# Feed-forward result read by VectorE straight from PSUM in the last residual sum of a decoder layer

## What is computed

```python
x = _layernorm(x + _L0_attn_ref(x, ...))
x = _layernorm(x + _L0_xattn_ref(x, ctx, ctx, decay))
x = _layernorm(x + _L0_ffn_ref(x, W_fc, W_proj))

def _L0_ffn_ref(x, W_fc, W_proj):
    h = jnp.einsum('bsd,hd->bsh', x, ternary(W_fc))      # 512 -> 2048
    h = jnp.square(jax.nn.relu(h))
    hn = h * rsqrt(mean(h * h) + eps)                    # over the 2048
    return jnp.einsum('bsh,dh->bsd', hn, ternary(W_proj))  # 2048 -> 512
```

## Time and profile before

| | |
|---|---|
| median of 3 runs | 1288.41 us (1281.94 to 1293.75) |
| the profiled execution | 1287.73 us |
| its span, first to last instruction | 1285.7 us |
| TensorE (PE) busy | 1116.7 us, 87% of the span |
| VectorE (DVE) busy | 941.3 us, 73% |
| ScalarE (ACT) busy | 587.3 us, 46% |
| GpSimd (POOL) busy | 202.5 us, 16% |
| mean granted TensorE clock | 0.941 of 2.4 GHz |

### The profile page before, as it was taken

One profiled execution on the slowest core, in us unless ns is written; L12 is line 12 of the kernel. 1 busy time (PEld: TensorE's weight loads), 2 busy tenths in 40 slices (PEclk: granted clock), 3 DMA queues, 4 the chain that ended last, 5 costly groups with the idle time before them and its releaser, 6 DMA issues.

```text
span 1285.7 us, 21818 instructions
## 1 busy us (share of the span) xinstructions
PE 1116.7 (87%) x7424; PEld 879.2 (68%) x7424; DVE 941.3 (73%) x1932; ACT 587.3 (46%) x906; POOL 202.5 (16%) x202
## 2 busy tenths in 40 slices
PE   5988989898989897724589997998989989999995
PEld 4766767676767674413368786787877878778784
DVE  4238788888888896788458678586795867958746
ACT  4323243434343434011166554565565665655673
POOL 3111003030303132300430201003020030110000
PEclk8989999999999998856699998999999999999998
DMA  7466666777767577633561021101210112100001
GB/s 277 126 180 148 170 145 203 148 196 155 192 151 198 120 196 218 163 86 62 184 222 41 1 66 66 51 14 65 65 65 31 34 65 65 65 1 1 33 1 66
DMA packets 184339, 139.40 MB, mean 108 GB/s; under 512 B 140128, under 2 KB 152416, under 8 KB 180192
## 3 DMA queue, kind: packets, MB, share of 16 engines
q1 hardware_dynamic: 113120, 113.57, 32.8%
q10 hardware_dynamic: 71168, 25.17, 7.9%
HBM read 82.09 MB, written 52.43 MB: 105 GB/s over the span
## 4 chain that ended last, share of the span: by engine, by line
PE 50%; DVE 26%; ACT 9%; issue 6%; DMA 5%; SPq 3%; POOL 1%; ACTq 0%; DVEq 0%; POOLq 0%
PE ps_s L779 13%; PE ps_f L765 12%; PE ps_f L569 9%; PE ps_o L716 5%; PE ps_s L591 5%; DVE w_pos L1204 3%; SPq L386 2%; DVE row_sum L1130 2%; ACT h_sb L1000 2%; DMA w_in<-in_L_ffn_W_fc 2%; DVE h_acc L1330 2%; DVE sc L1113 2%; DVE sc L1120 2%; DVE row_max L1116 2%; DVE st L1107 1%
## 5 line engine op out<-in xcount | busy, mean ns | idle before, releaser
L765 PE MATMUL ps_f<-x2h,w 128*128 128x512 f32 x512 | 203.9, 398 | 0.2 <-issue 0.2
L779 PE MATMUL ps_s<-w,hh 128*128 128x512 f32 x500 | 201.5, 403 | 0.0
L765 PE MATMUL ps_f<-x2l,w 128*128 128x512 f32 x512 | 199.9, 390 | 0.0
L779 PE MATMUL ps_s<-w,hl 128*128 128x512 f32 x500 | 199.6, 399 | 0.0
L1319 DVE TENSOR_TENSOR hl<-h_sb,hh 128x512 fp32r<-128x512 f32 x128 | 92.1, 720 | 116.0 <-ACT hh L1004 114.3
L569 PE MATMUL ps_f<-xth,wh 128*128 128x512 f32 x384 | 156.9, 409 | 1.6 <-DVE xtl L1099 1.6
L569 PE MATMUL ps_f<-xth,wl 128*128 128x512 f32 x384 | 151.8, 395 | 0.0
L569 PE MATMUL ps_f<-xtl,wh 128*128 128x512 f32 x384 | 151.7, 395 | 0.0
L591 PE MATMUL ps_s<-qbd,k 128*32 128x128 f32 x2048 | 128.1, 412 | 19.8 <-DVE o_sb L1163 14.1
L994 ACT ACTIVATE r_sb<-ps_f 128x512 f32<-128x512 f32 x128 | 76.2, 595 | 124.8 <-PE ps_f L765 124.7
L1514 POOL TENSOR_TENSOR xb<-xb,bob 128x512 f32<-128x512 f32 x32 | 66.3, 2101 | 411.4 <-DMA xb<-in_x 411.4
(11 more groups left out here) (145 smaller groups left out, 1941.8 us busy)
## 6 DMA issues: line engine op xcount, KB each, us to landing
xa<-in_x SPq DMA_DIRECT2D x8, 1024.0 KB, 5.6
q_scr<-f_sb ACTq DMA_DIRECT2D x32, 256.0 KB, 2.4
k_scr<-f_sb ACTq DMA_DIRECT2D x32, 256.0 KB, 3.9
v_scr<-f_sb ACTq DMA_DIRECT2D x32, 256.0 KB, 3.0
w_scr<-w_st SPq DMA_DIRECT2D x32, 256.0 KB, 4.9
k<-k_scr SPq DMA_DIRECT2D x8, 1024.0 KB, 5.5
qbd<-q_scr SPq DMA_DIRECT2D x128, 64.0 KB, 3.5
v<-v_scr SPq DMA_DIRECT2D x64, 128.0 KB, 6.0
```

Source lines behind the costliest of these rows:

```text
L765: last = nc.tensor.matmul(ps_f[:, j % 2, :], w1[:, k, j * P:(j + 1) * P], xx[:, k, :], start=(k == 0 and xx is x2h), stop=(k == KC - 1 and ...
L779: last = nc.tensor.matmul(ps_s[:, t, :], a[:, j % 4, t * P:(t + 1) * P], w2[:, j, :], start=(j == 0 and a is hh), stop=(j == HC - 1 and a ...
```

## The change

ScalarE's four copies of `ps_s` to `res` at the end of each pass are dropped, and with them the semaphore `f2_ev`. VectorE's `add_hidden` reads `ps_s` itself. For this it waits for the last down group of the pass before (`f2_ps`, in the last pass `f2_tile` of the tile) and, at tile 0, for the write of the output before that one (`out_wr`). TensorE's first down group of a pass waits for the four sums (`o1_done`) in place of the four copies. The four sums of a pass stand in steps 0 (tiles 0 and 1) and 1 (tiles 2 and 3) in place of steps 1 and 3. Pass 1 is written out on all engines, and the loop runs over passes 2 to 5.

```diff
@@ phase_b, and the same on SyncE's queue
             body(0, True, False, True)
-            with eng.Fori(1, NSB - 2) as i:
+            body(1, True, True, True)
+            with eng.Fori(2, NSB - 2) as i:
                 body(i, True, True, True)
@@ TensorE, down
                 if j == 0 and later(i):
-                    pe.wait_ge(f2_ev, at(i, TT, 0))
+                    pe.wait_ge(o1_done, at(i, TT, 0))
@@ ScalarE, end of body_b
-                if prep:
-                    act.wait_ge(f2_ps, at(i, HC, HC))
-                if fin:
-                    act.wait_ge(out_wr, 16 * i)
-                for t in range(TT):
-                    if not prep:
-                        act.wait_ge(f2_tile, t + 1)
-                    nc.scalar.activation(res[:, t, :], ps_s[:, t, :], ACT.Copy).then_inc(f2_ev, 1)
@@ VectorE, add_hidden
-                v.wait_ge(f2_ev, at(i, TT, t + 1))
-                nc.vector.scalar_tensor_tensor(out=res[:, t, :], in0=res[:, t, :], scalar=h_rs[:, t:t + 1],
+                if isinstance(i, int) and i == NSB - 1:
+                    v.wait_ge(f2_tile, t + 1)
+                elif t == 0:
+                    v.wait_ge(f2_ps, at(i, HC, HC))
+                if t == 0 and not (isinstance(i, int) and i == 0):
+                    v.wait_ge(out_wr, 16 * i)
+                nc.vector.scalar_tensor_tensor(out=res[:, t, :], in0=ps_s[:, t, :], scalar=h_rs[:, t:t + 1],
                                                in1=x2c[:, t, :], op0=ALU.mult, op1=ALU.add).then_inc(o1_done, 1)
@@ VectorE, body_b
-                        if j in (1, 3):
-                            add_hidden(i - 1, j - 1)
-                            add_hidden(i - 1, j)
+                        if j in (0, 1):
+                            add_hidden(i - 1, 2 * j)
+                            add_hidden(i - 1, 2 * j + 1)
```

More of the change, by code:

```diff
@@ L263, in program @@
         f2_ps = sem("f2_ps")
-        f2_ev = sem("f2_ev")
         f2_tile = sem("f2_tile")
@@ L515, in _ @@
             body_b(0, True, False)
-            with sp.Fori(1, NSB - 2) as i:
+            body_b(1, True, True)
+            with sp.Fori(2, NSB - 2) as i:
                 body_b(i, True, True)
```

## The result

| | before | changed |
|---|---|---|
| median of the compared runs | 1285.31 us | 1304.59 us |
| lowest to highest | 1281.94 to 1293.75, 4 runs | 1301.74 to 1307.99, 4 runs |
| profiled execution | 1287.73 us | 1303.08 us |
| its span | 1285.7 us | 1301.2 us |
| mean granted TensorE clock | 0.941 | 0.938 |

The ratio is 1.0135, 95% interval 1.0099 to 1.017: the change makes the kernel 1.35% slower (the two medians stand 19.3 us, 1.5%, apart). The forecast was 1300.0 us, 1293 to 1306.

A forecast was written before the change was run, and what follows sets the result against it. A feed-forward pass was taken to last TensorE's work plus its waits, the one long wait being 3.2 us at step 15. 1287.7 + 6.2 (`kv` at six borders) + 6.0 (last pass) = 1299.9, so 1300 us, range 1293 to 1306.

The forecast's parts named there:

- The two waits of the sum: TensorE's waits on `kv` at six borders, 6.2 us, and on the sums in the last pass, 6.0 us with clock loss.
- What it removes: 32 ScalarE copies of 0.6 us: worth 0.1 us per border, nothing at the very end.
- The read from PSUM at 0.74 us: VectorE's sums reading PSUM: 0.74 us each, as from SBUF, bounds 0.68 and 0.80; 1.7 us over seven borders either way.
- The down group of a loop pass: Step 3: sums done at 900.71, TensorE comes at 900.89, so the new wait is hidden by 0.2 us.
- `kv` 1.1 and 0.9 us late at six borders: Step 3's context transposes wait for `kv`: 1.1 us at four loop borders, 0.9 at two straight ones, 6.2 us.
- The wait at step 15 unchanged: TensorE's 3.2 us wait for `x2l` stays, as VectorE's chain is started by TensorE's step 11 and shifts along.
- The last pass: TensorE's first down group waits 4.1 us for the sums, then loses 1.9 us to a lower clock: 6.0 us.
- gone 0.20: Rival: pass 1 loses its collision of VectorE with GpSimd's bias additions, total 1295.3 us; chance 0.20.
- one more 0.12: Rival: one more collision of VectorE and GpSimd, in another pass, total 1304.5 us; chance 0.12.
- Absorbed: Rival: step 15's wait ends by something not tied to TensorE, six borders cost nothing, 1293.7 us; chance 0.07.
- faster: Rival: fewer sums in step 3 bring `x2l` forward, 2.8 us in five passes, 1.2 in the sixth, 1278.5 us; chance 0.04.
- clock at each border: Rival: 1.1 us more waiting lowers the clock at six borders, 1.8 us each, 1311 us; chance 0.05.

The follow-up runs named there:

- The kernels with the copies dropped and the costs taken away: Changed kernel, `kv` ahead of `h_sq`, GpSimd's bias additions held: ratio 0.9954; with output norm at step 4 and copies kept for pass 6 too: 0.9757.
- changed with the additions held: Changed kernel with GpSimd's four bias additions held until VectorE's last `x2l`: 1295.92 us, ratio 1.0062 to the kernel before.
- the kernels with `kv` in time: Among them the changed kernel with context square `kv` ahead of `h_sq` at step 2 on ScalarE: 1295.82 us, ratio 1.0067.
- one wait on GpSimd: Kernel before with GpSimd's four bias additions held until the last `x2l`: 1278.60 us, ratio 0.9925.
- work moved out of the chain ahead of the long wait: Kernel before, VectorE's output norm moved from step 12 to step 4: 1265.57 us, ratio 0.9829; with GpSimd's bias additions held too: 1258.39 us, 0.9736.

## Why the prediction was right, point by point

The forecast was 1300.0 us, +12.2 on the profiled 1287.7; the changed kernel took 1304.6, and the profiled execution 1303.1, +15.4. The two waits of the sum came out as foreseen in place, cause and nearly in size. What is missing is the collision that was a rival, and one term that nothing in the sum stood for. How near the number came is in part luck: these two together cost 6.3 us in the profiled execution, and a first phase that happened to be 2.2 us shorter hid a part of them. The likelier outcome of the forecast, within one per cent at 0.58, did not come; slower by more, at 0.38, did, by 1.35% (0.99 to 1.7).

- **What it removes: nothing gained.** Right. The kernels with the copies dropped and the costs taken away are 0.1 us or so a pass from their counterparts, on the slower side (77.26 to 77.19; 81.7 to 81.8 for 81.6 to 81.7).
- **The read from PSUM at 0.74 us.** Right: 32 sums from PSUM take 732 to 752 ns, median 735, and 736 from SBUF before. The Trainium skill, page "Perfetto Trace Analysis", section "Optimizing Scalar/DVE Operations", would by an estimate from its figures make each 65 ns longer. The trace does not agree.
- **The down group of a loop pass: hidden by 0.2 us.** Right, 0.3 (the last sum ends at 896.83, the group starts at 897.15). With the sums back in steps 1 and 3 it is 5.5 us of waiting.
- **`kv` 1.1 and 0.9 us late at six borders, 6.2 in all.** Right in each link (`h_acc`, `h_sq`, `kv`, transposes) and nearly in size: 1.0 in the loop, 0.7 to 0.8 in the two straight passes, 5.5 in all. Counted from the mean square, `kv` ends at 13.92 (899.91) where the forecast had it at 14.04 (903.78).
- **The wait at step 15 unchanged.** The wait was, at 3.20. Its price was not: in passes 2 and 4 the slow clock behind it lasted some 6 us instead of 4, 1.3 us more each. This term is missing from the sum. It was there in the kernels with a late `kv` (changed; the sums moved alone; changed with the additions held; changed with the copies kept for pass 6), in about every second of their uncollided passes, and in none of the uncollided ones of the kernels with `kv` in time. The windows show what differs: in all these passes the clock fell 0.73 to 1.04 us before the wait ended, and the stretch at 0.50 was 6.8 us long; in the uncollided passes with the short stretch, 3.4 us, it fell between 0.65 us before the end and 1.4 us behind it; and in two, of 80.06 and 80.02 us, it didn't fall. In the kernel before, that place moved by some 0.3 us from pass to pass (0.50, 0.81, 1.10 and 1.37 us behind the end in passes 2 to 5), and a pass that is 1.0 us longer moves it otherwise. So the late `kv` need not act on the clock over the 60 us of even work between the two; that it only shifts where the fall comes fits all these rows, but no edit tested it. Nor does a longer stretch need a late `kv` where there is a collision: in pass 3 of the kernel with pass 1 written out alone TensorE was busy 78.98 us for 77.58 in its pass 2.
- **The last pass: 4.1 of waiting and 1.9 of clock, 6.0.** 5.8: a delay of 4.2 (4.01 of it idle) and 4.0 us at 0.60, which is 1.6.
- **The collision, gone 0.20, one more 0.12.** One more came, by 3.7 us, though in another way: that of pass 1 went and two came in passes 3 and 5, so both rivals came at once and the second twice. That writing out pass 1 would move the landing in all the later passes was not seen: I wrote that this adds code and leaves the work per pass, and put no price on it. By itself it costs 0.66% (0.36 to 0.97), half of what the whole change does. The chances leaned towards the collision gone; the rows had one collision in five passes to lose and four to gain, which speaks for the other.
- **Absorbed, faster, clock at each border.** None came. The moved sums did not bring `x2l` forward, and the clock at the 0.8 us waits stayed up.

The sum by what was measured: 5.5 + 5.8 + 3.7 + 2.6 = 17.6 us, less the 2.2 ahead of the first mean square, which no step of the forecast spoke of.

## What to carry to other kernels

Before an edit frees a buffer later than before, list what is queued on the reading engine behind the moved work; here the reader was in time, and the work behind it (one `h_acc` sum, two engines on) set the price. Where a helper engine shares a port with the critical one, tie its start to an event instead of to a landing: one wait on GpSimd was worth 0.75% on the kernel before, took the scatter of tenths of a microsecond out of the comparison, and together with work moved out of the chain ahead of the long wait 2.6%. And a change that drops work from an engine with room should be expected to gain nothing and be judged by its waits alone.

## What the runs showed of the hardware that was not expected

- **Who gets the port.** In the collided passes VectorE's instructions with two SBUF inputs took 1.77 us for 0.68, and its `TENSOR_SCALAR` group 2.92 for 1.92; `x2l`, with one input in PSUM, took 0.68 in the midst of GpSimd's additions (874.02, above). The Trainium skill, page "SBUF — State Buffer", section "Who interferes with whom", says that a VectorE instruction with at most one SBUF input doesn't contend outside the two-port modes, and one with two does; these rows agree on both. The fourth of the `TENSOR_SCALAR` instructions, which has one tensor input in SBUF, was held up too (1.5 to 1.6 us for 0.54); no run shows in which mode it ran. When GpSimd came 0.03 us too late it stood behind a whole run of VectorE instructions that followed each other at once, 10.7 to 11.1 us for four additions of 1.3 each.
- **Writing out a pass moves transfers.** The same instructions in a straight pass ahead of a shorter loop brought GpSimd's start some 0.2 us nearer to the issue of its load in the loop passes that follow (5.06 to 5.10 us with that edit alone, 5.31 to 5.53 before).
- **The slow stretch behind a wait is not fixed by the wait.** After waits of 3.20 and 3.21 us, windows of four microseconds had a granted clock of 0.57 before and of 0.50 after, and the matmuls behind the wait were slow for about 4 and about 6 us; behind waits of 3.20 and 3.22 us in two other kernels the clock stayed at 1.00. A wait of one length thus cost its own length and up to 3 us more, or nothing more. After the waits of 1.4 us with the output norm at step 4 the granted clock stayed at 1.00.
- **The first phase.** The first mean square started between 715.9 and 726.3 us in kernels that hardly differ up to there (the bias additions are worth 2.2 us in the first wait). A single profiled execution says little about differences of a few microseconds in the whole span; the passes, cut at fixed instructions, agree to 0.1 us or so where neither a collision nor the slow stretch differs.
